# A decoder layer on one core: the first expert weights ahead of the third row broadcast, and the copy of a routed tile's result one unit earlier in ScalarE's program

## What is computed

```python
x = x + _L0_attn_ref(_layernorm(x), ...)      # state-space mixer: 1024 channels, 16 states
x = x + _L0_xattn_ref(_layernorm(x), ...)     # gated MLP whose factors are rounded to 8-bit integers
x = x + _L0_ffn_ref(_layernorm(x), ...)       # 16 experts, 2 per token, and a shared expert
```

## Times and profile before

| | us |
|---|---|
| median of 3 runs | 1636.22 (1634.85 to 1637.94) |
| the profiled execution, device time | 1631.51 |
| its span | 1629.8, granted TensorE clock 0.952 |
| TensorE busy | 1406.2 (86% of the span) |
| VectorE busy | 1323.2 (81%) |
| GpSimd busy | 1036.9 (64%) |
| ScalarE busy | 799.3 (49%) |
| scan stages begin (first decay) | 411.1, 776.9, 1141.2 |
| last scan of these stages ends | 665.0, 1030.7, 1394.4 |
| routed visits of the scan stages | 492 to 641, 857 to 1007, 1222 to 1371 |
| late stage, last copy of a result | 1608.2 to 1608.8 |

### The profile page before, as it was taken

One profiled execution on the slowest core, in us unless ns is written; L12 is line 12 of the kernel. 1 busy time (PEld: TensorE's weight loads), 2 busy tenths in 40 slices (PEclk: granted clock), 3 DMA queues, 4 the chain that ended last, 5 costly groups with the idle time before them and its releaser, 6 DMA issues.

```text
span 1629.8 us, 19427 instructions
## 1 busy us (share of the span) xinstructions
PE 1406.2 (86%) x5462; PEld 817.8 (50%) x5462; DVE 1323.2 (81%) x2196; ACT 799.3 (49%) x1365; POOL 1036.9 (64%) x672
## 2 busy tenths in 40 slices
PE   7597678999899899999899899999899999647994
PEld 4333223444555565444665565444555664336783
DVE  4589999688899999798899999798899999773212
ACT  3676444257544765247545765247545664131131
POOL 0299999103999898403999898403999898323001
PEclk9889899999899999999899999999899999868997
DMA  3550000413536783614537682614546783601984
GB/s 119 230 194 26 1 0 1 168 52 131 190 133 217 212 244 104 220 46 160 191 129 225 214 242 97 218 46 163 194 137 196 220 242 103 228 26 53 349 332 138
DMA packets 94074, 252.14 MB, mean 155 GB/s; under 512 B 11024, under 2 KB 11152, under 8 KB 88848
## 3 DMA queue, kind: packets, MB, share of 16 engines
q1 hardware_dynamic: 86688, 229.93, 42.0%
q0 software_dynamic: 5120, 16.78, 3.1%
q10 hardware_dynamic: 2160, 4.19, 0.8%
HBM read 207.87 MB, written 42.99 MB: 154 GB/s over the span
## 4 chain that ended last, share of the span: by engine, by line
PE 30%; DVE 17%; issue 11%; POOL 9%; ACT 3%; DMA 1%; DVEq 0%; POOLq 0%; ACTq 0%; SPq 0%
PE bank L1994 7%; DVE bank L1309 5%; POOL work L688 4%; PE bank L1836 3%; PE bank L2120 3%; PE bank L2023 3%; PE bank L1931 2%; PE bank L1926 2%; PE bank L1920 2%; PE bank L1970 2%; DVE work L1319 1%; PE bank L2015 1%; DVE pairs L1319 1%; POOL xs_dram L771 1%; DVE rr L1493 1%
## 5 line engine op out<-in xcount | busy, mean ns | idle before, releaser
L688 POOL TENSOR_TENSOR work<-du,BB 128x1024 f32<-128x1024 f32 x255 | 600.6, 2367 | 5.0 <-DVE work L1580 3.5
L980 ACT ACTIVATE bank<-delta,A_sb 128x512 f32<-128x512 f32 x512 | 349.2, 690 | 443.0 <-DVE pairs L1319 249.6
L1309 DVE TENSOR_TENSOR_SCAN bank<-bank,work 128x512 f32<-128x512 f32 x432 | 522.7, 1220 | 30.1 <-ACT bank L980 16.7
L1994 PEld LDWEIGHTS bank<-x3T,ew_up 128*128 128x128 f32 x1488 | 221.4, 196 | 80.2 <-issue 59.4
L1994 PE MATMUL bank<-x3T,ew_up 128*128 128x128 f32 (+1 forms) x1488 | 244.3, 311 | 11.3 <-DMA ew_up<-in_exp_w 9.1
L1319 DVE TENSOR_TENSOR pairs<-bank,CB 128x512 f32<-128x512 f32 x240 | 160.9, 670 | 3.0 <-PE bank L1931 2.5
L1319 DVE TENSOR_TENSOR work<-bank,CB 128x512 f32<-128x512 f32 x192 | 128.4, 669 | 0.0
L1926 PE MATMUL bank<-pairs,ident 128*128 128x512 f32 x160 | 89.2, 641 | 42.3 <-POOL pairs L741 17.8
L640 POOL TENSOR_TENSOR col<-col,halfpow 128x4 f32<-128x4 f32 (+1 forms) x8 | 7.8, 973 | 175.3 <-DVE col L1457 175.3
L2120 PE MATMUL bank<-wst,zg 128*128 128x512 f32 x256 | 117.0, 593 | 0.8 <-issue 0.8
L1849 PE MATMUL bank<-xT,wst 128*128 128x512 f32 x256 | 115.2, 597 | 0.0
(11 more groups left out here) (261 smaller groups left out, 2362.9 us busy)
## 6 DMA issues: line engine op xcount, KB each, us to landing
ew_up<-in_exp_w SPq DMA_DIRECT2D x93, 512.0 KB
ew_dn<-in_exp_w SPq DMA_DIRECT2D x93, 256.0 KB
hm<-xs_dram SPq DMA_DIRECT2D x69, 256.0 KB, 4.5
ys_dram<-x3T SPq DMA_DIRECT2D x69, 256.0 KB, 4.6
wst<-in_w_in SPq DMA_DIRECT2D x64, 256.0 KB, 2.6
BB<-bc_dram SPq DMA_DIRECT2D x16, 1024.0 KB, 4.8
CB<-bc_dram SPq DMA_DIRECT2D x16, 1024.0 KB, 6.9
wst<-in_out_w SPq DMA_DIRECT2D x32, 256.0 KB, 2.7
```

What stands on the lines that cost most here:

```text
L688: nc.gpsimd.tensor_tensor(dBu[:, k % CHUNK_SLOTS, :, :], du[:, j % 2:j % 2 + 1, :].broadcast_to([P, 2, T]), BB[:, n0:n0 + 2, :], ALU.mult) ...
L980: nc.scalar.activation(R[q % RING][:, :], delta[:, j, :], ACT.Exp, scale=A_sb[:, j, n:n + 1]).then_inc(S["da_ready"], 1)
L1309: V.tensor_tensor_scan(prod[c % (2 * PAIR_SLOTS)] if on_pool(q) else R[q % RING][:, :], R[q % RING][:, :], dBu[:, c // 2 % CHUNK_SLOTS, c ...
L1994: ins = mm(gu_bank(v)[:, part * n:(part + 1) * n], w[:, part * D + k * P:part * D + (k + 1) * P], rhs, start=(k == 0), stop=(k == KD - 1))
```

## The change

Two edits. The first moves `load_first_experts(b - 1)` ahead of the wait on `linkO` and of `broadcasts(b, 2)` on SyncE. The second sets `Y_COPY_BEHIND` to 8, so that the copy of routed visit r's result stands at unit 46 + 3r of ScalarE's loop and no longer at 47 + 3r.

```diff
-Y_COPY_BEHIND = 9
+Y_COPY_BEHIND = 8
...
                     weights("o", b, 0, 4)
+                    load_first_experts(b - 1)
                     wait(sp, "linkO", 3 * TT * b)
                     broadcasts(b, 2)
-                    load_first_experts(b - 1)
                     broadcasts(b, 3)
```

## The result

| | us |
|---|---|
| kernel before, median of 8 runs | 1638.17 (1634.75 to 1642.53) |
| changed kernel, median of 8 runs | 1627.19 (1625.10 to 1630.88) |
| ratio | 0.9935, 95% interval 0.9919 to 0.995 |
| profiled execution of the changed kernel | 1628.09, span 1626.3, granted clock 0.941 |

The change makes the kernel 0.65% faster, 10.6 us by the ratio (8 to 13 by its interval). Two repeats of the changed kernel against other runs of the kernel before gave 0.9955 and 0.9934.

The account below looks back on a forecast made before the run. TensorE was taken to set the ends of the first two scan stages and the late stage, VectorE's last scan the third; 1.7 + 1.7 + 2.7 + 0.9 = 7.0 us gave 1629.2, range 1626.5 to 1635.0.

Parts of the forecast that it names:

- The copy adds no wait to ScalarE: Routed visits, three scan stages: the down projection always ends before the decay now preceding the copy, closest 0.42 us; cost zero.
- (a): First scan stage, visit 2: TensorE's wait of 0.78 goes, and VectorE's 0.60 at its gate goes and stays gone.
- (b): First scan stage, visit 18: ScalarE's copy of the transposed rows limits TensorE's lead to 1.89 us; VectorE is then 1.20 ahead.
- (c): First two scan stages, unit 106: ScalarE's xT copy, now behind visit 20's result copy, leaves TensorE a lead of 1.27 us.
- (d): First two scan stages, at 636.76 in the first: TensorE's last wait, 0.42, goes, making it 1.69 us ahead.
- The third stage: No head there; VectorE's three waits for a sum go, and last scan, gathers and combine come 2.7 us earlier.
- The late tail: Late stage's last visit: visit 20's copy no longer starts behind the tanh, so TensorE's wait of 0.94 us goes.
- The first edit at nothing: Start of each scan stage: TensorE's 3.00 us wait for expert weights goes, counted as 0 since GpSimd's row decides.
- The rival of less lead: VectorE does not keep its 1.20 us, held by ScalarE or GpSimd; gain 3.4 us in all, 1632.8; chance 0.27.
- Nothing: The chain finds its way around each wait and only noise is left, 1636.2; chance 0.10.
- Lockstep: A late down projection makes the copy hold the decay and VectorE; both streams' pauses add up, +9.3 us, 1645.5; chance 0.06.
- The clock: VectorE waits for the first sums at the low clock, 3 us in each of three stages, 1638.4; chance 0.04.

Follow-up runs that it names:

- the kernel with the xT copy ahead: Changed kernel with ScalarE's copy to xT at unit 106 ahead of visit 20's result copy, not behind it; ratio 0.994 (0.9912 to 0.9967).
- the spare loads: Changed kernel with two further 512 KB transfers between the first experts' weights and the third broadcast in each scan stage; ratio 0.9969 (0.9951 to 0.9987).
- the held loads: Changed kernel, SyncE issuing the late stage's shared expert weights only after the third scan stage's eight gathers land; ratio 0.9899, median 1624.5.
- the lockstep kernel: Changed kernel with Y_COPY_BEHIND 7, not 8: the result copy in the down projection's own unit; ratio 1.0031 (1.0013 to 1.0049), median 1642.7.

## Why the prediction came out as it did

The forecast was 7.0 us of gain and a median of 1629.2; measured were 10.6 us by the ratio, 9.7 to 11.0 by the distances (less up to 0.7 behind the last scan), and 1627.2. The mechanism held at each step, and four terms of the sum were too small. The forecast started from three runs of before, whose median is 2.0 us under that of eight; from 1638.2 the same sum would have led to 1631.2, still in the range. So it is in part luck that the forecast time lies only 2.0 us from the measured one: the low start hid part of a gain that was 3.6 us too small.

- **The copy adds no wait to ScalarE.** Right for the scan stages, which is where I had compared: the list of the changed kernel has no wait of the copy at line 1043 for the down projection. The 0.42 us of room where it was closest were enough. The test with one unit more shows how little that is. For the late stage I had not looked, and there the copy does wait, 26.8 us in all where it was 2.6. That this cost nothing is not something the prediction had reasoned.
- **(a) VectorE's wait of 0.60 goes and stays gone.** Right; its gate comes 0.67 us earlier.
- **(b) The rows copy caps the lead.** Right in place: 0.55 us of wait at the transposes behind visit 18's copy. Mis-sized in VectorE's share: I had it 1.20 us ahead at the second gate, and it was 1.72 (616.73 instead of 618.59, less the 0.14 at unit 48). I had counted the two gates at their idle times, and each gave 0.07 to 0.10 more; and I had left out VectorE's product that waited 0.16 for TensorE at 595.7 (it came 0.25 earlier) and a crumb of 0.09 at the gate of 559.6. These 0.5 us pass on to all that follows.
- **(c) The xT copy caps it again.** Right in place, 0.56 us of wait. The lead there was 1.88 (630.15 to 628.12, less 0.14), and 1.27 was forecast: the same 0.5 us and 0.1 more. That it was a bound of the stage's end, the kernel with the xT copy ahead showed.
- **(d) and the end of the stage.** 2.5 us in each of the first two, 1.69 forecast: the 0.6 us from (b) and (c), and 0.63 rather than 0.42 at the last step.
- **The third stage.** 3.4 where 2.7 was forecast, with VectorE's three waits gone as said. The term was the sum of idle times as shown; each gate gave 0.07 to 0.10 us more than its idle time, the product's 0.16 (0.25 in effect) was left out here too, and 0.19 more came behind the last gate. Of TensorE's three waits one stayed, at 0.74 us and without effect on VectorE.
- **The late tail.** 1.3 where 0.94 was forecast. The rows of the changed kernel, the place of the earlier trace rows:

```profile
1599.92 1.02 PE L2023 MATMUL bank<-CB,etm 128*128 128x512 f32 x2
1600.78 1.05 PE L1994 MATMUL bank<-pairs,CB 128*128 128x128 f32 x8
1600.98 0.59 ACT L1039 COPY zg<-bank 128x512 f32<-128x512 f32 x1 [1.48 <-PE bank L2023]
1601.71 1.10 PE L2023 MATMUL bank<-CB,etm 128*128 128x512 f32 x2
```

The down projection follows the gate and up half at once. From the down projection before it, this takes 1.79 us where it took 2.93, so 1.14 with the wait of 0.94. The step ahead gave 0.20 more: there TensorE had started 0.14 us behind the end of a copy (1602.16) as well, an idle time too short for the list.

- **The first edit at nothing.** Right, and for the reason given. The room of 1.85 us for chunk 4 was too wide, it is 1.05 in this stage: the five loads were done at 417.6 as forecast minus the shift of this execution, but the two broadcasts behind them took 5.9 us, not 5.2.
- **The rival of less lead** (0.27): wrong, VectorE kept its lead. **Nothing**: wrong. **Lockstep**: not in this kernel, but one unit on. I had priced it at 9.3 us against the kernel before by adding up TensorE's pauses in the scan stages. It was 4 to 5 us against the kernel before, and two thirds of what it costs against the changed kernel came from the late stage, where I hadn't looked for it.
- **The clock** (0.04): the low clock did come to the first sums behind the new pause, in the third stage:

```profile
1150.87 2.04 PE L1920 MATMUL bank<-pairs,ident 128*128 128x512 f32 x2 [3.04 <-POOL pairs L738]
1152.71 1.91 PE L1926 MATMUL bank<-pairs,ident 128*128 128x512 f32 x2
1154.42 1.91 PE L1931 MATMUL bank<-pairs,ident 128*128 128x512 f32 x2
```

Such a pair takes 1.02 us at 2.4 GHz; here the granted clock is 0.5, 1.2 GHz, from 1150.0 to 1156.8. Decay to unit 16 is still 39.34 us there, as before: nobody waited for these sums, which is what spoke against this rival. In the first stage the sums behind the same pause of 3.05 us ran at the high level. Of the 30 scan stages of the ten profiles with the first edit, six had the first sums at the low level, three of them behind a pause of 3.0 us and three behind one of 4.7, and without the spare loads the distance to unit 16 was 39.30 to 39.35 in all. The rule of the Trainium skill (TensorE: Matmul & The Clock Gate, Part 1), that an idle array falls back to the slow clock, agrees with these six stages.

- **What the prediction did not have.** The up to 0.7 us behind the eighth gather. I had the gathers on the third stage's chain, but took them to follow the scan at a fixed distance; the loads that run beside them hang on another engine's row, and the change moved that one further.

What stays open: how much the held loads bring beyond 3 us, why the scatter is slow in some executions only, what decides how long the clock stays low behind the last scan, and where the 0.19 us behind the third stage's last gate come from.

## What to carry to other kernels

When two streams are both nearly full, follow the lead of the one past each place where the other holds it, and add in the small waits of 0.1 to 0.2 us: they are passed on undiminished, as the large ones are not. An instruction on a queue that others share may move ahead as long as what stands behind it is not held past the time when it is wanted. It may even wait itself: 1.2 us at each visit of the late stage did no harm here, 2.4 us made each visit 0.55 us longer. The place to look for the harm is the stage in which nothing else covers it. And where a profile's span moves less than the medians, compare distances between the same rows of each stage before looking for a cause in the change.

## What the runs showed of the hardware

The granted clock in a stretch of short, broken TensorE work is not the same from one execution of a kernel to the next: 58.0 and 64.9 us at the low level in some 150 us of the changed kernel, with a length of 147.7 and 149.8 to 150.1; over all thirteen profiles 54.6 to 64.9 us, with 146.9 to 151.6. An indirect gather landed 3.6 us after its issue when the weight loads were held back (1396.50 to 1400.14). With four weight loads issued 0.67 to 0.69 us behind it, it took 5.3 to 6.0 (three profiles; the 5.3 is taken from the next gather's start), with them 0.33 to 0.35 behind 6.6 to 7.6 (seven profiles), and 8.3 with them 0.1 ahead (the lockstep kernel): the loads that were issued after it delayed it.
